# Two conditioned attention layers on one core: another hand-written order for the second layer, and another split of its stacking transfers

## The reference, cut to what matters

```python
xn = layer_norm(x) * norm_w + norm_b
q, k, v = xn @ q_w + q_b, xn @ k_w + k_b, xn @ v_w + v_b        # (8, 512, 16, 32)
att = softmax(einsum('bnhl,bmhl->bnmh', q, k) + (1 - mask) * -1e6, axis=2)
y = einsum('bnmh,bmhl->bnhl', att, v)
h = layer_norm(y) * (1 + scale) + shift                         # scale, shift from silu(emb) @ emb_w
out = x + silu(h) @ out_w + out_b
```

## Time and profile before

| | |
|---|---|
| median of 3 runs | 1455.05 us (1454.03 to 1459.29) |
| the profiled execution | 1455.05 us, of which its span is 1453.2 us |
| layer 1 | steps from about 544 us to 1415 us of the span |
| TensorE busy | 1366.8 us, 94% |
| DVE, ACT, POOL busy | 998.9, 809.8, 772.4 us |
| TensorE's granted clock, mean | 0.98 of 2.4 GHz |

### The profile page before, as it was taken

How to read it: one execution, slowest core, us unless ns; L and a number is a source line. 1 busy time by engine, 2 the same in 40 slices (tenths; PEclk the granted TensorE clock), 3 DMA queues, 4 the chain that set the end, 5 groups by cost and what they waited for, 6 DMA issues and landing times.

```text
span 1453.2 us, 20521 instructions
## 1 busy us (share of the span) xinstructions
PE 1366.8 (94%) x7040; PEld 965.2 (66%) x7040; DVE 998.9 (69%) x1958; ACT 809.8 (56%) x1417; POOL 772.4 (53%) x692
## 2 busy tenths in 40 slices
PE   6899999999999799999999999998999999999985
PEld 4688888888888675566665665665665666566543
DVE  5787887878879676657647746756655656746754
ACT  4454455455455535656647646746745755665562
POOL 0323343243333425558658667566666756846952
PEclk9999999999999899999999999999999999999997
DMA  9011121111222266546336336335434643633520
GB/s 329 28 39 58 37 94 46 50 63 33 95 80 81 73 204 222 163 140 187 102 118 200 119 116 186 121 109 185 135 117 136 177 124 117 181 117 108 167 74 30
DMA packets 82888, 172.93 MB, mean 119 GB/s; under 512 B 7240, under 2 KB 7240, under 8 KB 82784
## 3 DMA queue, kind: packets, MB, share of 16 engines
q1 hardware_dynamic: 82784, 171.62, 38.3%
HBM read 104.45 MB, written 67.14 MB: 118 GB/s over the span
## 4 chain that ended last, share of the span: by engine, by line
PE 72%; DVE 12%; DMA 5%; ACT 5%; POOL 2%; issue 2%; SPq 1%; POOLq 0%; DVEq 0%; ACTq 0%
PE ps L497 14%; PE ps L499 13%; PE ps L498 13%; PE ps L653 7%; PE ps L687 7%; PE ps L670 7%; PE ps L492 5%; DVE cT L1183 5%; DMA Ks<-mask_scratch 4%; PE ps L708 2%; PE ps L606 1%; ACT xTh L768 1%; ACT ps L770 1%; PE ps L585 1%; DVE ps L1154 1%
## 5 line engine op out<-in xcount | busy, mean ns | idle before, releaser
L1345 POOL TENSOR_TENSOR Pb<-Pb 128x512 f32<-128x512 f32 x376 | 471.6, 1289 | 207.2 <-PE ps L687 171.8
L907 ACT ACTIVATE Pb<-ps 128x512 f32<-128x512 f32 x512 | 278.9, 610 | 212.2 <-PE ps L670 153.8
L1183 DVE TENSOR_REDUCE cT<-ps 128x1 f32<-128x512 f32 x512 | 327.3, 683 | 98.0 <-PE ps L653 97.9
L653 PE MATMUL ps<-Ks,Qs 98*128 98x512 f32 x512 | 190.0, 414 | 11.3 <-DMA Ks<-mask_scratch 7.2
L670 PE MATMUL ps<-Qs,Ks 106*128 106x512 f32 x512 | 187.7, 414 | 2.1 <-DVE xTl L1042 1.7
L653 PEld LDWEIGHTS ps<-Ks,Qs 98*128 98x128 f32 x512 | 92.7, 188 | 83.8 <-DVE cT L1183 34.2
L670 PEld LDWEIGHTS ps<-Qs,Ks 106*128 106x128 f32 x512 | 95.0, 189 | 57.3 <-DVE cT L1183 16.4
L1269 POOL TENSOR_TENSOR rs<-ve,mhalf 128x4 f32<-128x4 f32 x32 | 33.0, 1032 | 180.8 <-DVE ve L1015 134.1
L1297 POOL TENSOR_TENSOR vt<-vt,qmx 128x512 f32<-128x512 f32 x32 | 33.7, 1055 | 163.0 <-DVE qmx L1107 163.0
L497 PE MATMUL ps<-xTh,Wh_k 128*128 128x512 f32 x256 | 109.7, 429 | 4.7 <-DVE xTl L1042 3.6
L497 PE MATMUL ps<-Wh_o,sTh 128*128 128x512 f32 x256 | 107.3, 419 | 2.8 <-DVE sTl L1162 2.8
(11 more groups left out here) (175 smaller groups left out, 2940.6 us busy)
## 6 DMA issues: line engine op xcount, KB each, us to landing
Qs<-stack_scratch SPq DMA_DIRECT2D x32, 768.0 KB
Ks<-stack_scratch SPq DMA_DIRECT2D x32, 768.0 KB
stack_scratch<-sg_q SPq DMA_DIRECT2D x32, 512.0 KB, 2.7
stack_scratch<-sg_k SPq DMA_DIRECT2D x32, 512.0 KB, 2.6
wr<-in_x SPq DMA_DIRECT2D x32, 256.0 KB, 4.5
x_scratch<-wr SPq DMA_DIRECT2D x32, 256.0 KB, 2.0
stack_scratch<-sg_q SPq DMA_DIRECT2D x32, 256.0 KB, 2.9
stack_scratch<-sg_k SPq DMA_DIRECT2D x32, 256.0 KB, 3.3
```

The lines of the kernel that those rows point to most:

```text
L653: e.matmul(bank[:], Qs[par][0:RX, j, t * 128:(t + 1) * 128], Ks[par][0:RX, j, :], start=True, stop=True).then_inc(s["S"], 1)
L907: e.activation(p_buf(n, m)[:, j, :], ps[bank_of["a", n, m, j]][:], ACT.Exp).then_inc(s["P"], 1)
L1183: e.tensor_reduce(nx[:, n % 2, j, t, 0:1], ps[bank_of["S", n, j, t]][:], AX.X, ALU.max, negate=True).then_inc(s["S_max"], 1)
L1345: e.tensor_tensor(acc[:, j, :], acc[:, j, :], p_buf(n, m)[:, j, :], ALU.add).then_inc(s["Ps_pool"], 1)
```

## The change

Three things change, and no arithmetic.

1. **PLAN for the quarters of layer 1.** All tracks get one start and one end by quarter; the `weave` that cuts tracks into pieces goes. `nxt` of step n+1 has no track of its own: it is the end of the track of `S`, and follows its last product at once. The `ty` track is one track in g = 0, the `o` and `v` tracks are two and four of that kind. Layer 0's entries stay.
2. **Scratch layout.** Before, SP writes the high part twice, so that the scratch holds the 96 stacked rows (two DMAs for q and two for k, 768 KB each), and reads them with one DMA each. After, one DMA writes high and low part once (512 KB), and three DMAs of 32 rows each (256 KB) read what a stack needs.
3. **Counts of semaphores** that follow from 2.

```diff
 PLAN = {
     "0k": ..., "0v": ..., "0q": ..., "0o": ...            (the same)
-    "att": ((0.155, 0.288, 0.383, 0.543, 0.682, 0.863), (0.002, 0.187, 0.345, 0.502, 0.66, 0.817), (0.071, 0.269, 0.468, 0.666, 0.865, 1.063), (0.001, 0.174, 0.347, 0.52, 0.693, 0.866)),
-    "tl": (None, (0, 0.632), (0.05, 0.807), (0.036, 0.479)),
-    "tlx": ((0.007, 0.493), None, None, None),
-    "ty": ((0, 0.707, 0.741), (0, 0.903, 0.943), (0, 0.936, 0.976), (0, 1.0, 1.15), (0, 1.02, 1.17)),
-    "S": ((0.405, 0.491, 0.578, 0.664, 0.727), (0.112, 0.301, 0.494, 0.687, 0.88), (0.186, 0.255, 0.333, 0.505, 0.611), (0.235, 0.351, 0.387, 0.466, 0.582)),
-    "nxt": ((0.851, 0.99), (0.899, 0.993), (0.846, 0.866), (0.849, 0.88)),
-    "q": ((0.219, 0.3, 0.411), (0, 0, 0.02), (0.116, 0.149, 0.292), (0, 0.011, 0.139)),
-    "k": ((0.445, 0.495, 0.611), (0.271, 0.425, 0.531), (0.328, 0.478, 0.621), (0.206, 0.387, 0.568)),
-    "stack": ((0.722, 0.722), (0.758, 0.758), (0.742, 0.742), (0.983, 0.983)),
-    "nx": (None, (0.111, 0.885), None, None),
-    "tx": (None, (0.886, 1.181), None, None),
-    "o": ((1, 0, 0.176), (1, 0.87, 0.91), (2, 0.031, 0.088), (2, 0.844, 0.884)),
-    "v": ((2, 0.574, 0.744), (3, 0.482, 0.611), (3, 0.547, 0.697), (3, 0.568, 1.033)),
-    "we": ((0.807, 1.068), (0.364, 1.11), (0.262, 0.976), None),
+    "att": ((0.03, 0.83), (0.03, 0.83), (0.1, 0.97), (0.03, 0.83)),
+    "tl": (None, (0, 0.72), (0, 0.63), (0, 0.6)),
+    "tlx": ((0, 0.44), None, None, None),
+    "ty": ((0.55, 0.82), None, None, None),
+    "S": ((0.36, 0.78), (0.4, 0.91), (0.36, 0.78), (0.35, 0.85)),
+    "q": ((0.08, 0.36), (0.0, 0.13), (0.0, 0.3), (0.0, 0.3)),
+    "k": ((0.3, 0.6), (0.26, 0.57), (0.32, 0.54), (0.32, 0.6)),
+    "stack": ((0.76, 0.76), (0.8, 0.8), (0.78, 0.78), (0.8, 0.8)),
+    "o0": (None, (0, 0.1), (0, 0.17), None),
+    "o1": (None, (0.51, 0.81), (0.74, 0.92), None),
+    "nx": (None, (0, 0.55), None, None),
+    "tx": (None, (0.75, 1.13), None, None),
+    "v0": (None, None, (0.53, 0.7), (0.54, 0.78)),
+    "v1": (None, None, None, (0.56, 0.82)),
+    "v2": (None, None, None, (0.85, 1.0)),
+    "we": ((0.5, 1.0), (0.4, 1), (0.2, 0.9), None),
 }
...
     def max_parts(n):
-        return [("S", n, j, t) for j in X for t in X]
+        return [("S", n, j, t) for j in X for t in X] + [("nxt", n)]
...
             def qk(i, n, which):
...
-                    rows = qkd[par, which].rearrange("j (r s) n -> (j r) s n", s=3)
-                    first, other = ((0, 2), (1, 0))[which]
-                    e.dma_start(rows[:, first:first + 2, :], sg[name][:].bitcast(F32)).then_inc(s[f"st{name}{par}"], 16)
-                    e.dma_start(rows[:, other, :], sg[name][:, 0, :].bitcast(F32)).then_inc(s[f"st{name}{par}"], 16)
+                    e.dma_start(qkd[par, which].rearrange("s p n -> p s n"),
+                                sg[name][:].bitcast(F32)).then_inc(s[f"st{name}{par}"], 16)

             def stack(i, n):
...
-                for which, S_ in enumerate((Qs[par], Ks[par])):
-                    e.wait_ge(s[f"st{'qk'[which]}{par}"], 32 * (n // 2 + 1))
-                    e.dma_start(S_[0:RM, :, :].bitcast(F32),
-                                qkd[par, which].rearrange("j p n -> p j n")).then_inc(s[f"stack{par}"], 16)
+                for which, (S_, rows) in enumerate(((Qs[par], (0, 0, 1)), (Ks[par], (0, 1, 0)))):
+                    e.wait_ge(s[f"st{'qk'[which]}{par}"], 16 * (n // 2 + 1))
+                    for r, p in enumerate(rows):
+                        e.dma_start(S_[32 * r:32 * r + 32, :, :].bitcast(F32),
+                                    qkd[par, which, p].rearrange("(j r) n -> r j n", r=32)).then_inc(s[f"stack{par}"], 16)
```

More of the change, by code:

```diff
@@ L67, in weave @@
     live = []
-    for parts, *at in tracks:
+    for parts, a, b in tracks:
         steps = [(p, i) for p in parts for i in range(len(COST[p[0]]))]
         total = sum(COST[p[0]][i] for p, i in steps) or 1.0
[L71 to L77, removed]
         if steps:
-            live.append([marks, steps])
+            live.append([a, (b - a) / total, steps])
     while live:
[L81 to L84, removed]
+        t = min(live, key=lambda x: x[0])
+        p, i = t[2].pop(0)
+        order.append((p, i))
+        t[0] += COST[p[0]][i] * t[1]
+        if not t[2]:
             live.remove(t)
@@ L134, in the_order @@
     weave(o, ([("v", 8, t) for t in (1, 2, 3)], 0, 1), ([("ty", B - 1, c) for c in range(5)], 0, 0.7))
-    weave(o, (tiles("o", B - 1), 0, 1), (max_parts(0) + [("nxt", 0)], 0, 0.8))
+    weave(o, (tiles("o", B - 1), 0, 1), (max_parts(0), 0, 0.8))
     o.append((("narrow",), 0))
@@ L157, in the_order @@
             put("tlx", [("tl", n - 1), ("tlx", b - 1), ("ny", 8 + b - 1)])
+            put("ty", [("ty", 8 + b - 1, c) for c in range(5)])
         if n + 1 < N1:
             put("S", max_parts(n + 1))
-            put("nxt", [("nxt", n + 1)])
         if n + 2 < N1:
@@ L166, in the_order @@
             tracks.append((wpart(1, "o") if g == 0 else mpart(1, g - 1), *PLAN["we"][g]))
[L167 to L172, removed]
+        if g in (1, 2) and b >= 1:
+            put("o0", [("o", 8 + b - 1, 2 * g - 2)])
+            put("o1", [("o", 8 + b - 1, 2 * g - 1)])
         if g == 1 and more:
@@ L175, in the_order @@
             put("tx", tiles("tx", 8 + b + 1))
-        for t in X:
-            if more and PLAN["v"][t][0] == g:
-                tracks.append(([("v", 8 + b + 1, t)], *PLAN["v"][t][1:]))
+        if g == 2 and more:
+            put("v0", [("v", 8 + b + 1, 0)])
+        if g == 3 and more:
+            put("v0", [("v", 8 + b + 1, 1)])
+            put("v1", [("v", 8 + b + 1, 2)])
+            put("v2", [("v", 8 + b + 1, 3)])
         weave(o, *tracks)
@@ L267, in cond_two_layers @@
         md = nc.dram_tensor("mask_scratch", [2, B, T], F32, kind="Internal").ap()
-        qkd = nc.dram_tensor("stack_scratch", [2, 2, 4, RM, T], F32, kind="Internal").ap()
+        qkd = nc.dram_tensor("stack_scratch", [2, 2, 2, 128, T], F32, kind="Internal").ap()
         x1d = nc.dram_tensor("x1_scratch", [B, T, D], F32, kind="Internal").ap()
@@ L437, in stack_count @@
         def stack_count(n):
-            return 16 * sum(3 if c % NG < 2 else 2 for c in range(n % 2, n + 1, 2))
+            return 16 * sum(7 if c % NG < 2 else 6 for c in range(n % 2, n + 1, 2))
         def p_buf(n, m):
@@ L878, in qk @@
                     elif n == 1:
-                        e.wait_ge(s[f"st{name}0"], 32)
+                        e.wait_ge(s[f"st{name}0"], 16)
                     else:
-                        e.wait_ge(s[f"st{name}{(n - 1) % 2}"], 32 * ((n - 1) // 2 + 1))
+                        e.wait_ge(s[f"st{name}{(n - 1) % 2}"], 16 * ((n - 1) // 2 + 1))
                     e.activation(sg[name][:, 0, :], ps[bank_of["qk", n, which]][:], ACT.Identity,
```

## The result

The changed kernel takes 1496.85 us (median of 4, 1493.16 to 1501.53), the one before 1456.18 us beside it (median of 4). The ratio is 1.028, with a 95% interval of 1.0243 to 1.0317: slower by 40.7 us. The forecast was 1487 us, in a range of 1458 to 1525. The profiled execution has a span of 1491.7 us, against 1453.2.

What follows compares the result with a forecast made beforehand. TensorE was taken as the bound, but the first quarter as DVE's. Terms of 15 (first quarter), 4 (POOL), 6 (clock) and 7 (other quarters) gave 32 us on 1455: 1487 us, range 1458 to 1525.

Steps and rivals of the forecast that it cites:

- (a): First quarter (g = 0), ACT: copy of DEN after five exponentials, 2.6 us later; reciprocal starts at 6.4, not 3.9.
- (b): First quarter, DVE: second `ty` pair (1.5 us) stands ahead of the last maximum and `nxt`, no longer behind `nxt`.
- main term: First quarter, DVE's queue: lateness 7.2 against 5.0 us, 2.2 us more in each of seven batches, 15 us.
- (c): POOL: four additions wait behind the `ty` pairs, so DEN of the next quarter is 0.6 us late; 4 us in all.
- The transfers: Last quarter's stack goes out ahead of the load of x; 8.6 us of operand waits go into DVE's lateness; 0.
- small waits: First quarter before, DVE: about 13.5 us of work from 999 on, 15.0 with these waits.
- Rival 4: Stack reads of 32 rows are slow; at a quarter of the speed 1900 us; chance 0.02.
- The other quarters: g = 1 to 3: DVE's backlog delays `nxt`, 0.3 us a quarter, 7 us; bounds 0 and 96.
- Batch 0: b = 0: a product wait more or less in the early steps, set at 0.
- The clock: New first quarter: two gaps of about 2 us may bring lower-clock spells; bounds 0 and 20, 6 us taken.
- gap that the prediction expected at the exponential's bank: New first quarter: a score product waits about 2 us for the bank of an exponential behind `yb`'s normalising on ACT.

Runs made afterwards that it cites:

- run 8: Kernel before with one entry moved: the last quarter's stack stands ahead of SP's load of x; 1445.18 us, ratio 0.9949 to the kernel before.
- run 9: run 8's kernel with the copy of DEN moved behind five exponentials of g = 0; ratio 1.0059 to the kernel before, 16 us over run 8.
- run 10: run 8's kernel with DVE's first `ty` pair behind `nxt` in g = 0, not ahead; ratio 0.9966 to the kernel before.
- run 5: Changed kernel with (a) undone: the copy of DEN ahead of the exponentials again; 1473.63 us, ratio 1.0143 to the kernel before.
- run 6: Changed kernel with (b) undone: the second `ty` pair behind `nxt`; ratio 1.0316 to the kernel before.
- run 7: Changed kernel with (a) and (b) both undone; ratio 1.0156 to the kernel before.
- run 1: Changed kernel's order with the old scratch, writes and reads; median 1502.91 us, ratio 1.0301 to the kernel before.
- run 12: Kernel before, with old scratch, writes and order; only the reads come in three pieces of 32 rows; 1477.52 us, ratio 1.0145.
- Run 4: New scratch, new marks in g = 1 to 3 only, old ones in g = 0; 1472.53 us, ratio 1.0098 to the kernel before.
- run 11: Kernel before with the new scratch, writes and reads, and the last quarter's stack ahead of the load of x; ratio 0.996.

## Why the prediction came out

The number came out, and the main mechanism with it. The sum got there partly by errors that cancel: a cost that it left out, two terms that were too small, one that isn't seen, and a gain that it held for hidden. Offsets of the product of maxima and lengths of the rest of a batch, in us, each from batches with no spell in that stretch, read from TensorE's timelines as above (before: batches 1 to 6, as batch 7 has no load of x):

| | offset of the product of maxima | rest of the batch | a spell behind the maxima adds |
|---|---|---|---|
| before | 25.2 to 25.9 | 87.0 | 0 |
| run 8 | 24.3 | 87.0 | 0 |
| run 9, the copy late | 26.5 | 87.0 | 0 |
| run 10, the first `ty` pair behind | 23.0 | 88.6 | no case |
| changed | 28.1 | 87.9 | 1.3 |
| run 5, (a) undone | 26.1 | 87.9 | 1.3 |
| run 6, (b) undone | 26.6 | 90.2 | no case |
| run 7, both undone | 24.7 | 90.3 | no case |

**The main term was right, and its cause is shown.** The first quarter is DVE's, and the copy of DEN behind five exponentials starts DVE 2.0 to 2.4 us late (2.6 forecast). Undone it gives 20 us back (run 5), and done alone it costs 16 (run 9). Without a spell ahead of it, the offset went from a mean of 25.5 (five batches) to 28.1 (batch 3, and two batches of run 1), 2.6 for 2.8 forecast; 0.6 of that is product work that moved, so 2.0 us a batch are lateness, 14 us for 15.

**Step (b) holds in its quarter and not at the end.** The second `ty` pair does hold the product of maxima up by 1.45 us (28.1 against 26.6), but undoing it gives nothing back (runs 6, 7; run 10 for the first pair in the old order): the cast, POOL's subtraction and `o` are late next. The prediction named that chain for (c), and didn't ask it of (b). Against run 8, (a) and (b) together make 3.8 us; against the kernel before 1.2 of these are set off by the operand waits that go. Whether (b) costs anything with `o` at its old place was not run.

**Step (c)**, 0.6 us a batch, 4 in the sum: the additions end at 1048.56 and DEN starts at 1048.72 without a named wait. The order of events was met, the cost isn't seen.

**The transfers.** "They go, but only into DVE's lateness" failed: run 8 gains 7.4 us of 8.6 by removing the same waits. The prediction gave DVE 13.5 us of work in the quarter, "with small waits 15.0", and took the quarter to be DVE's alone. The small waits were DVE standing idle for TensorE's late score products, 1.6 us in batch 4. What I had taken as cover was the next link. (Of the 8.6 us, 1.4 lie in g = 1 of batch 6, and not in g = 0.) The Trainium skill's rule, "DMA: Bandwidth & Descriptors", section "Rules for kernel authors" (128 partitions and at least 1 MiB for the most bandwidth, coalesce small transfers), agrees with run 12 in direction; the 32-row pieces landed 0.4 us later. The 1.45% that they cost come mostly from where that landing came last and from the spells behind it. In the changed kernel the first read goes out 8.6 us ahead of the quarter, 7.3 earlier than before, and the pieces cost nothing that is seen (run 1). Rival 4 is out.

**The other quarters**, 7 us forecast. The rest of a batch is 0.9 us longer, without a spell, though by the prediction's count it holds 0.6 us of products less: 1.5 us of lateness a batch, 10 us in seven (an estimate from these two numbers). Named waits are only part: the wait for x transposed is 3.9 us in six batches. Run 4 has them at 20 us over run 11, 8.6 and more of it by a wait that the changed kernel doesn't have. Which of their marks make up the 10 stays open.

**Batch 0** was set at 0, and 4.7 us of the span's 38.5 lie there. Its wait for the maxima in g = 0 is 3.68 us for 2.17. No run tells the cause.

**The clock**, 6 us forecast. In the seven batches the kernel before has five spells: four behind the maxima, which cost nothing by the table, and one behind the wait for the mask rows, some 1.6 us. The changed kernel has nine: six behind the wait for the split of q, 1.0 to 1.3 each, and three behind the maxima, 1.3 each in the two batches where it can be read. That is some 9 us more (an estimate from these rows). The gap that the prediction expected at the exponential's bank was for the bank that DVE's split of q empties, that is (a) once more, and its spells go with it in run 5.

So the trace puts the 38.5 us of span down to 14 (forecast 15) in the first quarter, some 10 (7) in the others, some 9 (6) by the clock, 0 (4) by POOL, and 4.7 (0) in batch 0; the gain by the transfers is inside the first. A batch takes 117.4 us, and 117 were forecast.

**A version better than both** is run 8: one mark of the kernel before, 1445.18 us.

## What to carry to other kernels

When an order is written out by hand, look for the entry that starts a serial chain across engines once per outer iteration, and put it ahead of bulk work in every queue that it passes; here five exponentials' worth of queue decided half of a 2.8% loss. A wait shown ahead of an instruction isn't its price: ask what is late next, and compare the offsets of a few milestones from the start of the iteration instead. A wait that also starves the engine you hold for the bound is paid in full; "small waits" in that engine's own sum are the sign of it. Compare iterations of one run that differ in a spell of the lower clock before you call it free or dear. A mixture of an old and a new plan can make waits that neither has. A DMA's cost hangs on what was issued ahead of it in its queue: put the one with a near deadline in front of the one with a far deadline.

## What was not expected of the hardware

Pauses of TensorE of 1.8 to 2.0 us are followed by a clock of 0.5 in some batches and not in others of the same run: in the kernel before, that at 1014 us was and that at 1241 wasn't. What a spell costs depends on what stands behind it: it cost 0 in run 8, 1.3 in run 5 and 1.6 in run 12. Run 1's executions, from 1494.9 to 1507.6 us, have mean clocks of 0.971 at the one end and 0.964 at the other. Six DMA issues on SP's queue take 3.2 to 3.4 us, while the mask rows behind them land only 0.4 us later than behind two: most of the issue time lies beside the transfers.
